# Relation stage: the order in which VectorE compares the edges, copies the projections and copies the scores

## The chip, the cores and the metric

The kernel runs on one core of one Trainium2 chip. The metric is the device time of one execution in microseconds (us); lower is better. A core has TensorE (PE, with its weight loads shown apart as PEld), VectorE (DVE), ScalarE (ACT), GpSimd (POOL), the queue engine SyncE (SP), and 16 DMA engines. Each engine runs its own list of instructions in order, and they wait for each other through semaphores only.

## The reference, cut to what matters

A chain of four graph layers and four feed-forward layers is added onto x (1875 nodes, 256 features; 31875 edges). The change lies in the third of the eight, relational attention:

```python
def _L1_gnn_ref(x, W, attn_src, attn_dst, edge_index, edge_type):
    h_all = jnp.einsum('nf,rof->rno', x, W).reshape(r, n, h, d)      # r = 8 relations, h = 8 heads, d = 32
    h_src = h_all[edge_type, src]
    h_dst = h_all[edge_type, dst]
    scores = jnp.einsum('ehd,hd->eh', h_src, attn_src) + jnp.einsum('ehd,hd->eh', h_dst, attn_dst)
    scores = jnp.where(scores > 0, scores, NEG_SLOPE * scores)
    amax = jnp.maximum(jax.ops.segment_max(scores, dst, num_segments=n), 0.0)
    w = jnp.exp(scores - amax[dst])
    denom = jax.ops.segment_sum(w, dst, num_segments=n) + 1e-12
    w = w / denom[dst]
    msg = h_src * w[..., None]
    out = jax.ops.segment_sum(msg, dst, num_segments=n)
```

## The kernel before

The nodes lie in T = 15 tiles of P = 128. The edges, sorted by tile of their destination, lie in EC = 264 chunks of 128. `relational_attention` runs its parts one after the other: `layernorm`, `relation_scores` (the one that changes), a release of semaphores with a barrier of all engines, a read of one number, `relation_rows`, and then one of two ways of attending. The number, `o.unfit`, tells whether the edges are ordered so that the segment maximum can be taken by scans in order (`attend_in_order`); it is zero here.

`relation_scores` does two things that share nothing but the engines.

- **Scores of the nodes.** SyncE loads the weights `w` (2 MB) and the heads. TensorE multiplies them in 32 products (L1843) into `p_proj`; VectorE copies that to `proj` (L1880). Then for each of 15 node tiles TensorE makes `p_score` out of two products (L1851), two banks in turn, and VectorE empties a bank with two copies (L1887, L1888). A tile waits for the two copies of the tile before the last.
- **Order of the edges.** VectorE writes each edge's key into `spread` (L1876). TensorE turns it round in 26 windows (L1832), ScalarE copies the result to `turned` (L1861, seven copies), and TensorE picks the keys just outside each window into `p_near` (L1835, L1836). VectorE then compares neighbours in `turned`: which key is smaller than the one before it (L1883), the sum of those (L1891), which equals the one before it (`o.same`, L1892), four comparisons and two sums on 26 columns (L1894 to L1900), and the masks `o.first_run` (L1903) and `o.last_run` (L1904). Semaphore `counted` is raised after the sums; TensorE, behind its last score product, waits for it and adds the three sums over the lanes (L1855). VectorE copies that (L1906) and makes `o.unfit` of it (L1908).

The order of the work is the order in which each engine's instructions are written; no scheduler moves anything. `v.drain()` makes VectorE wait for its own writes. TensorE's list is: window turns, near keys, projections (after `w_in` and `heads_in`), scores (after `proj_ready`), sums (after `counted`). GpSimd makes an index row (L1821) and issues four scatters of the adjacency (L489); it issues 132 more in `relation_rows`, paced there by TensorE. SyncE's next load, the turned weights of `relation_rows` (L1941), stands behind the barrier.

Of the kernel before, what the change touches and what calls it, by code (L numbers as in the profile page):

```python
# [9 lines left out]
ALU = mybir.AluOpType  # L10
ACT = mybir.ActivationFunctionType
AX = mybir.AxisListType

P = 128
N = 1875
D = 256
T = (N + P - 1) // P
# [9 lines left out]
R = 8  # L27
HD, DH = 8, 32
# [1753 lines left out]
def relation_scores(nc, g, xt, w, attn_src, attn_dst, score_src, score_dst, o):  # L1782


    S2 = 2 * HD
    W, L, PADS = Windows.COUNT, Windows.LANES, Windows.PADS
    sets = [range(a, min(a + 4, W)) for a in range(0, W, 4)]
    with Phase(nc, "rel") as ph:
        w_sb = ph.sb("w", [P, R, 2, D])
        heads = ph.sb("heads", [P, 2, S2])  # L1790
        proj = ph.sb("proj", [P, 2, R, S2])
        p_proj = ph.ps("p_proj", [P, 2, R, S2])
        p_score = [ph.ps(f"p_score{b}", [P, 512]) for b in range(2)]
        blanked, heads_in, w_in = ph.sem("blanked"), ph.sem("heads_in"), ph.sem("w_in")
        proj_done, proj_ready, score_done, score_taken = (ph.sem(s) for s in ("proj_done", "proj_ready", "score_done", "score_taken"))
        chunk, lift = ph.sb("chunk", [P, EC + PADS]), ph.sb("lift", [P, EC])
        spread, turned = ph.sb("spread", [P, EC + PADS, HD]), ph.sb("turned", [L, W, P])
        drop_sum, near = ph.sb("drop_sum", [L, 3]), ph.sb("near", [L, 2, W])
# [64 lines left out]
        @block.vector  # L1863
        def _(v):
            nc.vector.memset(heads[:, :, :], 0.0).then_inc(blanked, 1)
            v.wait_ge(chunk_made, 1)
            nc.vector.tensor_scalar(lift[:, :], chunk[:, 0:EC], 1.0 / 1024, P + 0.5, ALU.mult, ALU.add)
            v.drain()
            nc.vector.scalar_tensor_tensor(lift[:, :], g.dst[:, :], 0.0, lift[:, :], ALU.is_lt, ALU.mult)
            nc.vector.memset(spread[:, 0:1, :], -5.0)  # L1870
            nc.vector.tensor_scalar(spread[:, EC + 1:EC + PADS, :], chunk[:, EC + 1:EC + PADS].unsqueeze(2).to_broadcast([P, PADS - 1, HD]),
                                    float(1 << 16), None, ALU.add)
            v.drain()
            nc.vector.scalar_tensor_tensor(lift[:, :], g.tile_of[:, :], float(P), lift[:, :], ALU.mult, ALU.add)
            v.drain()
            nc.vector.tensor_tensor(spread[:, 1:EC + 1, :], g.dst[:, :].unsqueeze(2).to_broadcast([P, EC, HD]),  # L1876
                                    lift[:, :].unsqueeze(2).to_broadcast([P, EC, HD]), ALU.add).then_inc(keyed, 1)
            nc.vector.memset(o.same[:, :, :], 0.0)
            v.wait_ge(proj_done, 1)
            nc.vector.tensor_copy(proj[:, :, :, :], p_proj[:, :, :, :]).then_inc(proj_ready, 1)  # L1880
            v.wait_ge(key_copied, len(sets))
            now, earlier = turned[:, :, 1:P], turned[:, :, 0:P - 1]
            nc.vector.tensor_tensor(o.first_run[:, :, 0:P - 1], now, earlier, ALU.is_lt)  # L1883
            for t in range(T):
                v.wait_ge(score_done, t + 1)
                both = p_score[t % 2][:, 0:R * S2].rearrange("p (r s) -> p r s", r=R)
                nc.vector.tensor_copy(score_src[:, t, :, :], both[:, :, 0:HD]).then_inc(score_taken, 1)  # L1887
                nc.vector.tensor_copy(score_dst[:, t, :].rearrange("p (r h) -> p r h", r=R), both[:, :, HD:S2]).then_inc(score_taken, 1)  # L1888
            v.wait_ge(neared, 1)
            nc.vector.tensor_copy(near[:, :, :], p_near[:, :, :])  # L1890
            nc.vector.tensor_reduce(drop_sum[:, 0:1], o.first_run[:, :, 0:P - 1], AX.XY, ALU.add)  # L1891
            nc.vector.tensor_tensor(o.same[:, :, 1:P], now, earlier, ALU.is_equal)  # L1892
            v.drain()
            nc.vector.tensor_tensor(crossed[:, 0, :], turned[:, :, 0], near[:, 0, :], ALU.is_lt)  # L1894
            nc.vector.tensor_tensor(crossed[:, 1, :], near[:, 0, :], near[:, 1, :], ALU.is_equal)
            nc.vector.tensor_tensor(o.joined[:, :, 0], turned[:, :, 0], near[:, 0, :], ALU.is_equal)
            nc.vector.tensor_tensor(o.joined[:, :, 1], turned[:, :, P - 1], near[:, 1, :], ALU.is_equal)
            v.drain()
            nc.vector.tensor_reduce(drop_sum[:, 1:2], crossed[:, 0, :], AX.X, ALU.add)
            nc.vector.tensor_reduce(drop_sum[:, 2:3], crossed[:, 1, :], AX.X, ALU.add)  # L1900
            v.drain()
            v.sem_inc(counted, 1)
            nc.vector.tensor_tensor(o.first_run[:, :, :], turned[:, :, :], turned[:, :, 0:1].to_broadcast([L, W, P]), ALU.is_equal)  # L1903
            nc.vector.tensor_tensor(o.last_run[:, :, :], turned[:, :, :], turned[:, :, P - 1:P].to_broadcast([L, W, P]), ALU.is_equal)  # L1904
            v.wait_ge(drops_added, 1)
            nc.vector.tensor_copy(total[:, :], p_total[:, :])  # L1906
            v.drain()
            nc.vector.tensor_reduce(o.unfit[:, :], total[:, :], AX.X, ALU.max)  # L1908
# [627 lines left out]
```

## Time and profile before

| | us |
|---|---|
| median of 3 runs | 4527.47 |
| lowest, highest run | 4523.1, 4533.64 |
| the profiled execution, its own time | 4526.65 |
| span of the profiled execution, first to last instruction | 4525.0 |
| `relation_scores` in it, from its first instruction to its last | 2270.3 to 2335.7 |
| TensorE busy in the whole span | 2865.0 |
| VectorE busy in the whole span | 2207.9 |

The profile shows one execution. A timeline row is a start, a duration and an instruction (or a merged run of like ones, x8); the brackets behind it say how long the engine had been idle and what it had waited for. The parts of the layer are closed by barriers, so a part's length is set by whichever engine ends last in it, and the next part starts for all engines together.

### The profile page before, as it was taken

Reading aid. Unit: us, or ns where it says so; the run is one execution under the profiler, and the core shown is the slowest. Engines: PE = TensorE matmul, PEld = TensorE weight load, DVE = VectorE, ACT = ScalarE, POOL = GpSimd, SP = SyncE. Lnnn points to the kernel's source line nnn. Section 1 sums busy time; section 2 is a strip of 40 time slices with the busy share of each in tenths; the row PEclk is TensorE's granted clock in tenths of the full one; section 3 lists DMA queues with packets and bytes.
Section 4 is the critical chain, followed back from the end, with each engine's and each line's share of the span. In section 5 each row is a group of like instructions: output and inputs, shape, how many; then the busy total and the mean of one; then the engine's idle time right before and its main releaser. Section 6 shows DMA issues by size and latency. Waiting matters only on the chain. (4 is left out here: it accounts for less than half of the span.)

```text
span 4525.0 us, 52039 instructions
## 1 busy us (share of the span) xinstructions
PE 2865.0 (63%) x16062; PEld 2374.0 (52%) x16063; DVE 2207.9 (49%) x4940; ACT 726.2 (16%) x1635; POOL 1870.5 (41%) x1982
## 2 busy tenths in 40 slices
PE   3566657775777667750568256767769639947492
PEld 2456545563565455540557123336758639936391
DVE  7566645554555545566246556771254421144213
ACT  1122112221222212210112000002210113300120
POOL 4566456664666366636315666711100020020212
PEclk8788877877777777875769566667979869968696
DMA  5733223332333233313423133317756459945693
GB/s 129 287 87 88 68 67 90 90 84 59 88 89 90 53 90 89 90 34 130 161 54 109 41 92 93 94 43 254 245 185 234 157 183 327 309 149 171 210 338 119
DMA packets 358089, 607.55 MB, mean 134 GB/s; under 512 B 82185, under 2 KB 240187, under 8 KB 355131
## 3 DMA queue, kind: packets, MB, share of 16 engines
q1 hardware_dynamic: 245816, 357.76, 24.3%
q0 software_dynamic: 88640, 214.25, 17.0%
q10 hardware_dynamic: 23363, 32.26, 2.0%
q8 instruction: 130, 2.13, 0.2%
q14 instruction: 140, 1.15, 0.1%
HBM read 508.28 MB, written 95.81 MB: 134 GB/s over the span
## 5 line engine op out<-in xcount | busy, mean ns | idle before, releaser
L831 POOL DMA_INDIRECT gine_got<-gine_table,src x1056 | 1017.4, 963 | 561.2 <-issue 271.4
L905 PE MATMUL gine_p_sum<-gine_hot,gine_got 128*128 128x128 f32 x4224 | 782.9, 330 | 204.5 <-issue 174.0
L905 PEld LDWEIGHTS gine_p_sum<-gine_hot,gine_got 128*128 128x128 f32 x4224 | 690.2, 240 | 289.8 <-issue 266.0
L957 DVE TENSOR_TENSOR gine_got<-gine_got,gine_p_edge 128x512 f32<-128x512 f32 x528 | 360.5, 683 | 601.5 <-DMA unpack_rows<-in_edge_rows 250.7
L916 ACT ACTIVATE gine_got<-gine_got 128x512 f32<-128x512 f32 x528 | 332.2, 630 | 1309.5 <-DVE gine_got L957 946.9
L940 DVE TENSOR_TENSOR stack_acc<-stack_acc,gine_p_sum 128x256 f32 x1056 | 437.6, 414 | 43.0 <-issue 1.5
L489 POOL DMA_INDIRECT adjacency<-value,place x264 | 280.3, 1062 | 390.3 <-POOLq L54 191.4
L892 PE MATMUL gine_p_edge<-gine_w_a,edge_space 128*128 128x256 bf16 x1056 | 329.1, 326 | 98.7 <-issue 94.1
L893 PE MATMUL gine_p_edge<-gine_w_b,edge_space 128*128 128x256 bf16 x1056 | 328.7, 325 | 98.9 <-issue 85.8
L1416 PE MATMUL ffn_p_h<-ffn_xt,ffn_w 128*128 128x128 f32 x2864 | 347.7, 280 | 1.7 <-DVE ffn_xt L1468 0.5
L1416 PEld LDWEIGHTS ffn_p_h<-ffn_xt,ffn_w 128*128 128x128 f32 x2864 | 337.5, 196 | 4.6 <-issue 2.5
L1428 PE MATMUL ffn_p_y<-ffn_w,ffn_ht 128*128 128x256 f32 x1432 | 328.6, 380 | 4.1 <-DMA ffn_w<-in_L_ffn_w 4.1
L2302 PE MATMUL inorder_p_sum<-edge_space,inorder_hot 128*128 128x265 f32 x528 | 240.2, 572 | 132.3 <-DVE edge_space L2375 86.8
L2267 POOL DMA_INDIRECT edge_space<-h_table,hrow x264 | 272.7, 1033 | 123.3 <-issue 76.4
L1487 DVE TENSOR_TENSOR ffn_y<-ffn_p_y,ffn_b 128x256 f32<-128x256 f32 x112 | 47.5, 424 | 547.1 <-PE ffn_p_y L1428 547.1
L1682 PE MATMUL gcn_p_out<-gcn_h,gcn_a 128*128 128x256 f32 x1350 | 299.3, 380 | 0.0
L1453 ACT ACTIVATE ffn_ht<-ffn_p_h,ffn_b 128x128 f32<-128x128 f32 x716 | 204.2, 368 | 527.3 <-PE ffn_p_h L1416 527.2
L1428 PEld LDWEIGHTS ffn_p_y<-ffn_w,ffn_ht 128*128 128x128 f32 x1432 | 263.7, 190 | 37.7 <-DMA ffn_w<-in_L_ffn_w 6.2
L1682 PEld LDWEIGHTS gcn_p_out<-gcn_h,gcn_a 128*128 128x128 f32 x1350 | 254.4, 191 | 33.0
L1202 POOL IOTA route_e_idx<- 128x8 f32 (+1 forms) x3 | 0.4, 135 | 569.8 <-POOLq L54 569.8
L2302 PEld LDWEIGHTS inorder_p_sum<-edge_space,inorder_hot 128*128 128x128 f32 x528 | 114.5, 260 | 228.6 <-issue 225.4
L842 DVE TENSOR_TENSOR gine_hot<-iota_free,dst 128x512 f32<-128x512 f32 x264 | 181.6, 688 | 42.2 <-issue 36.9
(399 smaller groups left out, 3365.4 us busy)
## 6 DMA issues: line engine op xcount, KB each, us to landing
gcn_a<-adjacency SPq DMA_DIRECT2D x270, 320.0 KB
ffn_w<-in_L_ffn_W SPq DMA_DIRECT2D x74, 1024.0 KB
ffn_w<-in_L_ffn_w SPq DMA_DIRECT2D x60, 1024.0 KB
ffn_w<-in_L_ffn_w SPq DMA_DIRECT2D x90, 512.0 KB
adjacency<-zero_row ACTq DMA_DIRECT2D x3, 7200.0 KB
gine_got<-gine_table,src POOLq DMA_INDIRECT x1056
h_table<-score_rows SPq DMA_DIRECT2D x15, 1056.0 KB
edge_space<-dst_lines ACTq DMA_DIRECT2D x3, 2816.0 KB
```

Of the source, the lines that this page charges most:

```text
L489: pool.indirect_dma_start(self.tables[c % 2], bass.IndirectOffsetOnAxis(ap=self.place[:, c:c + 1], axis=0), self.value[:, c:c + 1], None). ...
L831: pool.indirect_dma_start(got[:, c % RING, :], None, table, bass.IndirectOffsetOnAxis(ap=rows[:, c:c + 1], axis=0)).then_inc(gathered[c % ...
L892: nc.tensor.matmul(edges, g.attrs_t[:, 2 * p + k, :], w_a[:, :], start=True, stop=False)
L893: ins = nc.tensor.matmul(edges, g.attrs_t[:, 2 * p + k, :], w_b[:, :], start=False, stop=True)
L905: ins = nc.tensor.matmul(p_sum[q % NB][:, k * D + half * P:k * D + (half + 1) * P], got[:, d % RING, half * P:(half + 1) * P], hot[:, d % ...
L916: nc.scalar.activation(got[:, a:a + 2, :], got[:, a:a + 2, :], ACT.Relu).then_inc(msg_ready, 1)
L940: nc.vector.tensor_tensor(into, into, p_sum[d // 2 % NB][:, d % 2 * D:(d % 2 + 1) * D], ALU.add).then_inc(added, 1)
L957: nc.vector.tensor_tensor(both, both, p_edge[p % NB][:, :], ALU.add).then_inc(summed, 1)
L1416: ins = nc.tensor.matmul(p_h[n % 2][m // 4][:, m % 4, :], w1_sb[:, n % 2, k, m * P:(m + 1) * P], xt[:, n % 2, k, :], start=(k == 0), stop= ...
L1428: ins = nc.tensor.matmul(p_y[n % 2][:, 0:D], ht[:, n % 2, m, :], w2_sb[:, n % 2, m, :], start=(m == 0), stop=(m == m_all - 1))
L1682: ins = nc.tensor.matmul(p_out[d][:, 0:D], a[:, n % RA, d * P:(d + 1) * P], h[:, t, :], start=(t == 0), stop=(t == T - 1))
L2302: nc.tensor.matmul(p_sum[c % SUMS][:, 0:WIDE], hot[:, c % HOTS, :], got[:, c % HELD, :], start=True, stop=True).then_inc(agg_done, 1)
```

## The change

In VectorE's list of `relation_scores`, the comparisons, sums and masks (L1883, L1890 to L1904) now stand directly behind the memset of `o.same` (L1878), ahead of the copy of the projections (L1880) and of the 30 score copies (L1887, L1888). Inside the moved block three things differ: a `drain` stands between L1883 and the sum over it, the sum and the equality come ahead of the wait for `neared`, and the copy of `p_near` stands behind that wait. No instruction is added or taken away except for that drain. No other engine's list changes.

```diff
             nc.vector.memset(o.same[:, :, :], 0.0)
-            v.wait_ge(proj_done, 1)
-            nc.vector.tensor_copy(proj[:, :, :, :], p_proj[:, :, :, :]).then_inc(proj_ready, 1)
             v.wait_ge(key_copied, len(sets))
             now, earlier = turned[:, :, 1:P], turned[:, :, 0:P - 1]
             nc.vector.tensor_tensor(o.first_run[:, :, 0:P - 1], now, earlier, ALU.is_lt)
+            v.drain()
+            nc.vector.tensor_reduce(drop_sum[:, 0:1], o.first_run[:, :, 0:P - 1], AX.XY, ALU.add)
+            nc.vector.tensor_tensor(o.same[:, :, 1:P], now, earlier, ALU.is_equal)
+            v.wait_ge(neared, 1)
+            nc.vector.tensor_copy(near[:, :, :], p_near[:, :, :])
+            v.drain()
...
+            v.sem_inc(counted, 1)
+            nc.vector.tensor_tensor(o.first_run[:, :, :], turned[:, :, :], turned[:, :, 0:1].to_broadcast([L, W, P]), ALU.is_equal)
+            nc.vector.tensor_tensor(o.last_run[:, :, :], turned[:, :, :], turned[:, :, P - 1:P].to_broadcast([L, W, P]), ALU.is_equal)
+            v.wait_ge(proj_done, 1)
+            nc.vector.tensor_copy(proj[:, :, :, :], p_proj[:, :, :, :]).then_inc(proj_ready, 1)
             for t in range(T):
                 v.wait_ge(score_done, t + 1)
                 both = p_score[t % 2][:, 0:R * S2].rearrange("p (r s) -> p r s", r=R)
                 nc.vector.tensor_copy(score_src[:, t, :, :], both[:, :, 0:HD]).then_inc(score_taken, 1)
                 nc.vector.tensor_copy(score_dst[:, t, :].rearrange("p (r h) -> p r h", r=R), both[:, :, HD:S2]).then_inc(score_taken, 1)
-            v.wait_ge(neared, 1)
-            nc.vector.tensor_copy(near[:, :, :], p_near[:, :, :])
-            nc.vector.tensor_reduce(drop_sum[:, 0:1], o.first_run[:, :, 0:P - 1], AX.XY, ALU.add)
-            nc.vector.tensor_tensor(o.same[:, :, 1:P], now, earlier, ALU.is_equal)
...
             v.wait_ge(drops_added, 1)
             nc.vector.tensor_copy(total[:, :], p_total[:, :])
```

VectorE's list around the copy of the projections, before (`rel_proj` is that copy, `rgat_in_score_src` and `rgat_in_score_dst` are the score copies, 15 of each, `rel_turned` the turned keys):

```order
L1876 TENSOR_TENSOR rel_spread<-dst,rel_lift 128x2112
L1878 MEMSET rgat_same_run 96x3354
L1880 COPY rel_proj<-rel_p_proj 128x256
L1883 TENSOR_TENSOR rgat_first_run<-rel_turned 96x26x127
L1887 COPY rgat_in_score_src<-rel_p_score 128x64
L1888 COPY rgat_in_score_dst<-rel_p_score 128x64
```

The same place now, from the memset on:

```order
L1876 TENSOR_TENSOR rel_spread<-dst,rel_lift 128x2112
L1878 MEMSET rgat_same_run 96x3354
L1881 TENSOR_TENSOR rgat_first_run<-rel_turned 96x26x127
L1883 TENSOR_REDUCE rel_drop_sum<-rgat_first_run 96x1
L1884 TENSOR_TENSOR rgat_same_run<-rel_turned 96x26x127
L1886 COPY rel_near<-rel_p_near 96x52
L1888 TENSOR_TENSOR rel_crossed<-rel_turned,rel_near 96x26
L1889 TENSOR_TENSOR rel_crossed<-rel_near 96x26
L1890 TENSOR_TENSOR rgat_joined<-rel_turned,rel_near 96x26
L1891 TENSOR_TENSOR rgat_joined<-rel_turned,rel_near 96x26
```

The projection copy has moved down behind this block. The rest of the block and the copy, as they now stand on VectorE:

```order
L1893 TENSOR_REDUCE rel_drop_sum<-rel_crossed 96x1
L1894 TENSOR_REDUCE rel_drop_sum<-rel_crossed 96x1
L1897 TENSOR_TENSOR rgat_first_run<-rel_turned 96x3328
L1898 TENSOR_TENSOR rgat_last_run<-rel_turned 96x3328
L1900 COPY rel_proj<-rel_p_proj 128x256
L1904 COPY rgat_in_score_src<-rel_p_score 128x64
L1905 COPY rgat_in_score_dst<-rel_p_score 128x64
```

Five long instructions (L1881, L1883, L1884, L1897, L1898) now stand ahead of the copy instead of none. The end of VectorE's list in this stage, before:

```order
L1899 TENSOR_REDUCE rel_drop_sum<-rel_crossed 96x1
L1900 TENSOR_REDUCE rel_drop_sum<-rel_crossed 96x1
L1903 TENSOR_TENSOR rgat_first_run<-rel_turned 96x3328
L1904 TENSOR_TENSOR rgat_last_run<-rel_turned 96x3328
L1906 COPY rel_total<-rel_p_total 1x3
L1908 TENSOR_REDUCE rgat_unfit<-rel_total 1x1
```

And now:

```order
L1904 COPY rgat_in_score_src<-rel_p_score 128x64
L1905 COPY rgat_in_score_dst<-rel_p_score 128x64
L1907 COPY rel_total<-rel_p_total 1x3
L1909 TENSOR_REDUCE rgat_unfit<-rel_total 1x1
L54 UNCONDITIONAL_BRANCH
```

Nothing but the copy of the sums and the final maximum stands between the last score copy and the end of the stage.

## Rows read from the trace of the kernel before

**Rows 1.** The page's head: the span of the profiled execution.
```profile
span 4525.0 us, 52039 instructions
```
**Rows 2.** Timeline up to the projections: start us, us, engine, line, operation, [idle before].
```profile
2275.31 2.85 DVE L1878 MEMSET rgat_same_run<- 96x3354 f32 x1 [0.65 <-issue]
2278.92 1.46 ACT L1861 COPY rel_turned<-rel_p_key 96x512 f32<-96x512 f32 x3 [0.25 <-PE rel_p_key L1832]
2292.03 0.46 PE L1836 MATMUL rel_p_near<-ident,rel_spread 128*96 128x1 f32 x2
2292.35 13.81 PE L1843 MATMUL rel_p_proj<-rel_heads,rel_w 128*128 128x16 f32 x64
2306.20 0.42 DVE L1880 COPY rel_proj<-rel_p_proj 128x256 f32<-128x256 f32 x1 [28.04 <-PE rel_p_proj L1843]
2306.54 3.58 DVE L1883 TENSOR_TENSOR rgat_first_run<-rel_turned 96x3302 f32<-96x3302 f32 x1
```
**Rows 3.** Timeline of the score products and their copies.
```profile
2306.68 2.08 PE L1851 MATMUL rel_p_score<-rel_proj,rgat_in_xt 128*128 128x128 f32 x8 [0.52 <-DVE rel_proj L1880]
2310.45 9.28 PE L1851 MATMUL rel_p_score<-rel_proj,rgat_in_xt 128*128 128x128 f32 x52 [1.69 <-DVE rgat_in_score_dst L1888]
2312.56 0.23 DVE L1887 COPY rgat_in_score_src<-rel_p_score 128x64 f32<-128x64 f32 x1 [0.50 <-PE rel_p_score L1851]
2313.41 0.23 DVE L1887 COPY rgat_in_score_src<-rel_p_score 128x64 f32<-128x64 f32 x1 [0.50 <-PE rel_p_score L1851]
2317.44 0.23 DVE L1887 COPY rgat_in_score_src<-rel_p_score 128x64 f32<-128x64 f32 x1 [0.31 <-PE rel_p_score L1851]
2319.76 0.23 DVE L1887 COPY rgat_in_score_src<-rel_p_score 128x64 f32<-128x64 f32 x1 [0.31 <-PE rel_p_score L1851]
```
**Rows 4.** Timeline of the stage's end: the comparisons and what waits for them.
```profile
2320.03 0.20 DVE L1890 COPY rel_near<-rel_p_near 96x52 f32<-96x52 f32 x1
2320.15 3.58 DVE L1891 TENSOR_REDUCE rel_drop_sum<-rgat_first_run 96x1 f32<-96x3302 f32 x1
2323.65 3.58 DVE L1892 TENSOR_TENSOR rgat_same_run<-rel_turned 96x3302 f32<-96x3302 f32 x1
...
2327.98 0.17 DVE L1900 TENSOR_REDUCE rel_drop_sum<-rel_crossed 96x1 f32<-96x26 f32 x1
2328.23 0.09 PEld L1855 LDWEIGHTS rel_p_total<-rel_drop_sum,ones 96*1 96x1 f32 x2 [8.69 <-DVEq L1901]
2328.23 0.19 PE L1855 MATMUL rel_p_total<-rel_drop_sum,ones 96*1 96x3 f32 x2 [8.50 <-DVEq L1901]
2328.26 3.62 DVE L1903 TENSOR_TENSOR rgat_first_run<-rel_turned 96x3328 f32<-96x3328 f32 x1
2331.80 3.62 DVE L1904 TENSOR_TENSOR rgat_last_run<-rel_turned 96x3328 f32<-96x3328 f32 x1
2335.34 0.14 DVE L1906 COPY rel_total<-rel_p_total 1x3 f32<-1x3 f32 x1
```
**Rows 5.** Busy us by stretch: PE, PEld, DVE, ACT, POOL; granted clock, DMA share, GB/s.
```profile
2280.60:2306.20 25.60, 25.57 (x160) 25.45 (x159) 0.00 (x0) 0.00 (x0) 0.00 (x0) 0.57 0.00 1
2320.00:2336.00 16.00, 0.19 (x2) 0.09 (x2) 15.36 (x14) 0.00 (x0) 0.00 (x0) 0.56 0.00 0
2315.00:2316.00 1.00, 1.00 (x9) 0.86 (x8) 0.71 (x4) 0.00 (x0) 0.00 (x0) 0.97 0.00 0
2352.00:2353.00 1.00, 1.00 (x5) 0.83 (x4) 0.00 (x0) 0.00 (x0) 0.00 (x0) 0.69 0.00 0
```
**Rows 6.** Issue and landing of the load with which the next part starts.
```profile
score_wt<-in_L_gnn_W_turned SPq DMA_DIRECT2D x1, 2048.0 KB, 7.9
```
**Rows 7.** Timeline of the next part, `relation_rows`: its products, and one pause.
```profile
2347.43 6.27 PE L1980 MATMUL score_p_rows<-score_wt,score_x_tile 128*128 128x256 f32 x16 [19.01 <-issue]
2354.52 7.10 PE L1980 MATMUL score_p_rows<-score_wt,score_x_tile 128*128 128x256 f32 x32
2383.82 0.59 ACT L2021 COPY score_rows<-score_p_rows 128x512 f32<-128x512 f32 x1 [8.35 <-DMA gather_got<-cap_results,cap_source_i]
2384.46 3.78 PE L1980 MATMUL score_p_rows<-score_wt,score_x_tile 128*128 128x256 f32 x8 [6.15 <-ACT score_rows L2021]
```

More of the change, by code:

```diff
@@ L1883, in _ @@
             nc.vector.tensor_tensor(o.first_run[:, :, 0:P - 1], now, earlier, ALU.is_lt)
[L1884 to L1888, printed above, removed]
+            v.drain()
+            nc.vector.tensor_reduce(drop_sum[:, 0:1], o.first_run[:, :, 0:P - 1], AX.XY, ALU.add)
+            nc.vector.tensor_tensor(o.same[:, :, 1:P], now, earlier, ALU.is_equal)
             v.wait_ge(neared, 1)
             nc.vector.tensor_copy(near[:, :, :], p_near[:, :, :])
-            nc.vector.tensor_reduce(drop_sum[:, 0:1], o.first_run[:, :, 0:P - 1], AX.XY, ALU.add)
-            nc.vector.tensor_tensor(o.same[:, :, 1:P], now, earlier, ALU.is_equal)
             v.drain()
@@ L1904, in _ @@
             nc.vector.tensor_tensor(o.last_run[:, :, :], turned[:, :, :], turned[:, :, P - 1:P].to_broadcast([L, W, P]), ALU.is_equal)
+            v.wait_ge(proj_done, 1)
+            nc.vector.tensor_copy(proj[:, :, :, :], p_proj[:, :, :, :]).then_inc(proj_ready, 1)
+            for t in range(T):
+                v.wait_ge(score_done, t + 1)
+                both = p_score[t % 2][:, 0:R * S2].rearrange("p (r s) -> p r s", r=R)
+                nc.vector.tensor_copy(score_src[:, t, :, :], both[:, :, 0:HD]).then_inc(score_taken, 1)
+                nc.vector.tensor_copy(score_dst[:, t, :].rearrange("p (r h) -> p r h", r=R), both[:, :, HD:S2]).then_inc(score_taken, 1)
             v.wait_ge(drops_added, 1)
```

## The prediction, made before the changed kernel had run

> **What bounds the kernel now.** I read the views in this order. The page's head gives the span, 4525.0 us [rows 1]; the layers run in sequence with barriers between their parts, so a part that ends earlier brings everything behind it forward. The reader should therefore look only at who ends last in this part. The timeline shows three stretches. In the first, VectorE has nothing to do: its memset ends at 2275.31 + 2.85 = 2278.16, and it then waits 28.04 us, until TensorE has finished the near keys and the projections at 2306.2 [rows 2]. In the second, TensorE makes the scores, to 2310.45 + 9.28 = 2319.73, with a pause of 1.69 us [rows 3]. In the third, VectorE alone works through its comparisons until it copies the sums at 2335.34 [rows 4]. The busy time by stretch says the same from the side of resources: from 2280.60 to 2306.20 TensorE is busy all of the time and VectorE, ScalarE, GpSimd and the DMA engines none of it; from 2320 to 2336 VectorE is busy 15.36 of 16 us and the others next to nothing [rows 5]. So the third stretch is bound by work whose data has been there for long: the keys were copied at 2278.92 + 1.46 = 2280.38, the near keys were ready at 2292.03 + 0.46 = 2292.49 [rows 2].
>
> **What the moved block costs in its new place.** It starts at 2280.4. The first comparison takes 3.58 (to 2284.0), the added drain and the sum another 3.6 (2287.6; 3.58, of which the row behind overlaps 0.08), the equality 3.5 (2291.2) [rows 2, 4]. Then comes the one wait that stands in a new place, for the near keys: VectorE stands 1.3 us, to 2292.5, and nobody waits for it there, since TensorE's next 13.8 us are projections that need nothing of VectorE. The near copy takes 0.2. The six small instructions end 0.92 us behind the equality (2327.98 + 0.17 less 2323.65 + 3.58), so 2293.7. The two masks take 2331.80 + 3.62 - 2328.26 = 7.2, to 2300.9 [rows 4]. The projections are complete at 2306.2. The cover is thus 5.3 us longer than what it hides, and I cost the block at nothing. If the cover failed, each microsecond past 2306.2 would delay the projection copy and with it all scores, one for one. The drain waits only for the comparison that the sum reads; no row shows one there, but the small instructions behind each other with drains between them (0.92 us in all) bound it at a few tenths, and the 5.3 us hold that. GpSimd, ScalarE and SyncE have no instruction that is moved past or held up: their DMAs and copies of this part are issued ahead of the block, and none waits for `counted`.
>
> **Term A, the scores.** Before, the first comparison (3.58 us) stood between the projection copy and the first score copy, so TensorE filled its two banks and paused 1.69 us [rows 3]. That pause goes. What becomes of the clock decides the rest. TensorE's granted clock was at its lower level, 1.2 GHz, from before the scores until about 2315.06 (the stretch 2315 to 2316 shows 0.97, so 0.06 us of it were at half) and then at 2.4 GHz [rows 5]. A tile took 0.85 us before the rise (2312.56 to 2313.41) and 0.58 after it (four tiles from 2317.44 to 2319.76) [rows 3]. The rise came 4.6 us after TensorE had taken up steady work again at 2310.45. In the next part it came 5.2 us after work began at 2347.43 (the stretch 2352 to 2353 shows 0.69, so the rise was at 2352.62) [rows 5, 7]. After the change the steady work begins at 2306.68, so I expect the rise at 2311.3 to 2311.9. By then 5.4 to 6.1 tiles are done, and the other 9.6 to 8.9 take 5.6 to 5.2 us, which gives 2316.9 to 2317.1. The same working applied to before gives 2319.46 against the 2319.73 of the row, so I add its 0.27: about 2317.3. Term A is 2319.73 - 2317.3 = 2.4 us. Bounds: if the rise stays where it was in time (2315.06), 9.9 tiles go at 0.85 and 5.1 at 0.58, the scores end at 2318.3, and A is 1.4; if the clock doesn't rise within the scores, fifteen tiles at 0.85 end at 2319.7 and A is 0. I take 2.4, by the two rises seen after steady work.
>
> A page has a say on this. The Trainium skill, "TensorE: Matmul & The Clock Gate", section "Part 1: The HAM clock gate", says that the clock rises after a time of sustained work, however many matmuls that is, and that the point varies from run to run. By it the removed pause counts double, as in my 2.4, but the rise isn't fixed to a few tenths; by row alone, with the rise left where it was, the term would be 1.4. No run yet shows which.
>
> **Term B, the tail.** Before, VectorE copied the sums 2335.34 - 2319.73 = 15.6 us after the last score product [rows 3, 4]. Now two score copies and the sum on TensorE lie between. The last score copy ended 0.38 us after the last product (2319.76 and 0.14 later its twin, of 0.21), and TensorE's sum, which before had waited 8.50 us for VectorE, takes 0.19 beside them [rows 3, 4]. The copy of the sums can start about 0.4 us behind the last product. Term B is 15.6 - 0.4 = 15.2 us.
>
> **What is late next.** After the stage everybody meets at the barrier, and the next part starts with a load of 2 MB that is issued behind it and takes 7.9 us to land [rows 6]. That load, the split of the scores and the products follow the barrier at fixed distances, and nothing was in flight from 2320 to 2336 that could still be late (0 GB/s) [rows 5]. So the whole chain shifts, and I find nothing that takes the 17.6 us back. TensorE's pause before the next part shrinks from 27.7 us (2319.73 to 2347.43) to about 12.5. The clock was down at its start before; since a pause of 6.15 us also left it down (eight matmuls in 3.78 us, against 32 in 7.10) [rows 7], I expect the same start and cost it at nothing, with 0.5 us either way.
>
> **The sum.** 2.4 + 15.2 = 17.6 us. On the profiled execution's own 4526.65 this gives 4509.05; on the median of the runs shown, 4527.47, which lies 0.8 above that, it gives 4509.9. That is 0.39% faster. With A at its bounds it would be 4510.9 or 4512.3.
>
> **The rivals.**
> - **A pause in the next part comes or goes.** ScalarE sat 8.35 us before one of its copies at 2383.82 for nothing that lies in this layer, TensorE stood 6.15 us for it, and ran the next eight matmuls in 3.78 us in place of 1.78 (8 of 7.10/32): 8.2 us in all [rows 7]. A pause of that kind may depend on how the engines stand to each other, and the start of the part shifts by 17.6 us. One more gives 4518.1, one fewer 4501.7; two more give 4526.3, which is no measurable change. Against it: all engines leave the same barrier in the same order as before. The Trainium skill, "Runtime: NRT & Kernel Launch", section "Instruction fetch mechanics", says that a taken branch whose target isn't in the window already loaded makes an engine wait for code. If these pauses are that, they hang on the loops' code, which the change leaves alone, and the time is the 4509.9 of the sum; the rows don't name the cause.
> - **The block is late.** If comparisons on VectorE run slower while TensorE is busy, the projection copy waits. The block has 17.9 us of long instructions; twice as long they would end it at about 2318.8, 12.6 us late, and 5.0 us would be left: 4522.5, no measurable change. Against it: L1883 ran beside the score products in the same 3.58 us as L1891 and L1892 ran alone [rows 2, 4].
> - **Slower: the clock in the next part.** Its 15 node tiles need 32 matmuls each: 7.10 us at 2.4 GHz, and 15.1 at the eight-in-3.78 pace, so a tile at half clock costs 8.0 us more [rows 7]. If the shorter pause ahead of the part kept the clock low longer, from 2.2 tiles on (17.6 / 8.0) the change would lose; four tiles give 4509.9 + 32 = 4541.9, slower. For it: the clock did fall while TensorE was busy (0.57 granted from 2280.60 to 2306.20) [rows 5], so work alone doesn't hold it. Against it: it rose within 5.2 us of this kind of matmul [rows 5, 7].
>
> **How the numbers follow.** The forecast with its variants of A, 4509.9 to 4512.3: 0.73. One pause fewer, 4501.7: 0.07. One more, 4518.1: 0.09. Two more, or the block late, 4522 to 4526: 0.07. Slower by the clock: 0.04. A difference under 0.2%, 9 us, can't be told from none here; that bound lies at 4518.4, so half of the 0.09 counts as no change once the runs' own spread of some 5 us is added. Faster: 0.73 + 0.07 + 0.05 = 0.85; same 0.11; slower 0.04. The range goes from 4501 to 4519: it takes in one pause more or fewer, and leaves out the last two cases.
>
> **What would show it.** In the profile after: the block lies between 2280 and 2301 with a wait of about 1.3 us for the near keys, and VectorE is idle again for about 5 us before the projection copy, which still stands 36 us behind the start of the stage. TensorE has no pause behind its second score tile and the clock rises near 2311.5, not 2315. The copy of the sums is at about 2317.7. The first product of the next part is near 2329.8, and from there each row stands about 17.6 us earlier to the end. The prediction is wrong if the projection copy moves, if the clock rises late or not at all, or if the parts behind the barrier don't keep their lengths.

## The result, and the profile after

| | before | after |
|---|---|---|
| median, us (8 runs each) | 4525.28 | 4507.47 |
| lowest, highest, us | 4513.83, 4533.64 | 4498.66, 4520.04 |
| ratio after to before, 95% interval | | 0.997 (0.9956 to 0.9984) |
| the profiled execution, own time, us | 4526.65 | 4511.05 |
| span of the profiled execution, us | 4525.0 | 4509.4 |

The changed kernel is faster by about 0.3%: the whole interval of the ratio lies below 1. The medians differ by 17.8 us; the ratio's interval, on 4525.28, says 7 to 20 us. The forecast was 4509.9, a ratio of 0.9961.

The starts of VectorE's instructions at the borders of the parts, those of its barriers included, show where the time went in the two profiled executions (us, worked out from the traces):

```
part                                   before     after   difference
everything ahead of relation_scores    2270.4    2268.9         -1.5
relation_scores                          66.2      48.3        -17.9
barrier, split of the scores              4.1       4.1          0.0
relation_rows (from the split's end)    233.7     229.5         -4.2
to attend_in_order                        3.5       4.0         +0.5
attend_in_order                         433.8     434.2         +0.4
divide_into to the end of the span     1513.3    1520.4         +7.1
```

Only the second row is the change. The others add up to +2.3, and their own spread is larger than that, as the runs below show.

The timeline of the changed kernel up to the projections, VectorE's rows but for one (the small instructions left out):

```profile
2278.92 3.60 DVE L1881 TENSOR_TENSOR rgat_first_run<-rel_turned 96x3302 f32<-96x3302 f32 x1 [2.25 <-ACT rel_turned L1861]
2282.59 3.59 DVE L1883 TENSOR_REDUCE rel_drop_sum<-rgat_first_run 96x1 f32<-96x3302 f32 x1
2286.10 3.58 DVE L1884 TENSOR_TENSOR rgat_same_run<-rel_turned 96x3302 f32<-96x3302 f32 x1
2290.86 13.81 PE L1843 MATMUL rel_p_proj<-rel_heads,rel_w 128*128 128x16 f32 x64
2291.04 0.21 DVE L1886 COPY rel_near<-rel_p_near 96x52 f32<-96x52 f32 x1 [1.35 <-PE rel_p_near L1836]
...
2292.27 3.62 DVE L1897 TENSOR_TENSOR rgat_first_run<-rel_turned 96x3328 f32<-96x3328 f32 x1
2295.81 3.62 DVE L1898 TENSOR_TENSOR rgat_last_run<-rel_turned 96x3328 f32<-96x3328 f32 x1
2304.71 0.42 DVE L1900 COPY rel_proj<-rel_p_proj 128x256 f32<-128x256 f32 x1 [5.29 <-PE rel_p_proj L1843]
```

The wait of 28.04 us before the projection copy [rows 2] has become three short ones, 2.25 for the keys, 1.35 for the near keys, 5.29 for the projections, with the block between them. The five long instructions take what they took before [rows 2, 4]. The stage's first VectorE instruction starts at 2268.86 here and at 2270.36 before, so the projection copy stands 35.84 us behind it before and 35.85 after: the block has delayed nothing. The projections themselves took 13.81 us, as before [rows 2].

The scores and the end of the stage, same view:

```profile
2305.19 10.44 PE L1851 MATMUL rel_p_score<-rel_proj,rgat_in_xt 128*128 128x128 f32 x60 [0.52 <-DVE rel_proj L1900]
...
2315.56 0.19 PE L1855 MATMUL rel_p_total<-rel_drop_sum,ones 96*1 96x3 f32 x2
2315.66 0.23 DVE L1904 COPY rgat_in_score_src<-rel_p_score 128x64 f32<-128x64 f32 x1
2315.80 0.21 DVE L1905 COPY rgat_in_score_dst<-rel_p_score 128x64 f32<-128x64 f32 x1
2315.94 0.14 DVE L1907 COPY rel_total<-rel_p_total 1x3 f32<-1x3 f32 x1
```

All 60 score matmuls (30 products, of which each leaves two records) are one run, where before there were two with 1.69 us between them [rows 3]. The 8.50 us that TensorE's sum waited and the 15.6 us of VectorE's tail [rows 4] are gone. Busy time by stretch (columns as in rows 5), the same 25.6 us as there and the second of the clock's rise:

```profile
2280.60:2306.20 25.60, 25.08 (x147) 24.98 (x147) 17.56 (x13) 0.00 (x0) 0.00 (x0) 0.54 0.00 1
2310.00:2311.00 1.00, 1.00 (x9) 0.86 (x7) 0.58 (x4) 0.00 (x0) 0.00 (x0) 0.92 0.00 0
```

VectorE, idle there before, is busy 17.56 us. The clock reached 2.4 GHz at about 2310.16 (0.92 of that microsecond), 5.0 us after the scores began.

### The profile page after: what moved, and what is told of

Same layout as the page of the kernel before. It is cut to its first block and busy times, and to the rows that moved or that the text cites. A ratio compares the mean times of both kernels' runs of the same rounds, so it can differ in the third digit from the quotient of the medians.

```text
span 4509.4 us, 52040 instructions
## 1 busy us (share of the span) xinstructions
PE 2857.9 (63%) x16062; PEld 2366.4 (52%) x16063; DVE 2208.4 (49%) x4940; ACT 726.0 (16%) x1635; POOL 1867.8 (41%) x1982
## 5 line engine op out<-in xcount | busy, mean ns | idle before, releaser
L892 PEld LDWEIGHTS gine_p_edge<-gine_w_a,edge_space 128*128 128x128 bf16 x1056 | 124.3, 118 | 150.8 <-issue 119.0
```

Of the source, the lines that this page charges most:

```text
L892: nc.tensor.matmul(edges, g.attrs_t[:, 2 * p + k, :], w_a[:, :], start=True, stop=False)
```

## The experiments

The runs of the experiments were made in four sets, beside which the kernel before had medians of 4496, 4490, 4494 and 4191 us (4525 beside the result above), so kernels of different sets are compared by their ratio to the kernel before, run beside them, and by times counted from the stage's first VectorE instruction. Kernels without an interval ran once.

### Term A: one mask back between the projection copy and the scores

```diff
-            nc.vector.tensor_tensor(o.last_run[:, :, :], turned[:, :, :], turned[:, :, P - 1:P].to_broadcast([L, W, P]), ALU.is_equal)
             v.wait_ge(proj_done, 1)
             nc.vector.tensor_copy(proj[:, :, :, :], p_proj[:, :, :, :]).then_inc(proj_ready, 1)
+            nc.vector.tensor_tensor(o.last_run[:, :, :], turned[:, :, :], turned[:, :, P - 1:P].to_broadcast([L, W, P]), ALU.is_equal)
```

> The changed kernel with one of its two masks (last_run, 3.62 us) put back between the projection copy and the first score copy; the rest of the block stays ahead. It tests term A alone. In the changed kernel the copy of the sums starts 47.1 us after the stage's first VectorE instruction. My theory (the pause goes, and the clock rises earlier because steady work starts earlier, 2.4 us together): TensorE pauses about 1.7 us after two tiles again, the clock rises about 4.6 to 5.2 us after the pause, and the copy of the sums starts at 49.5 (2.4 later). Rival (only the pause counts, the clock rises where it does in the changed kernel): 48.3 to 48.8. Rival (no effect, VectorE's copies catch up): 47.1.

Timeline of this kernel:

```profile
2287.40 0.43 DVE L1899 COPY rel_proj<-rel_p_proj 128x256 f32<-128x256 f32 x1 [8.82 <-PE rel_p_proj L1843]
2287.74 3.61 DVE L1900 TENSOR_TENSOR rgat_last_run<-rel_turned 96x3328 f32<-96x3328 f32 x1
2287.88 2.08 PE L1851 MATMUL rel_p_score<-rel_proj,rgat_in_xt 128*128 128x128 f32 x8 [0.52 <-DVE rel_proj L1899]
...
2291.68 9.71 PE L1851 MATMUL rel_p_score<-rel_proj,rgat_in_xt 128*128 128x128 f32 x52 [1.72 <-DVE rgat_in_score_dst L1905]
```

The pause is back, 1.72 us after eight matmuls. The copy of the sums came 51.8 us behind the stage's start, not 49.5: the projections themselves were 1.6 us later than in the changed kernel (37.5 against 35.85), as they were in most of the later runs, whatever stood behind them. Counted from the projection copy the distance to the copy of the sums is 14.3 us, where the theory had 13.65 and the rival without the clock 12.45 to 12.95. In the eight runs that have the scores and the sums in the changed order it lies between 10.7 and 11.7 (11.2 in the profile above), so one long instruction in that place costs 2.6 to 3.6 us, more than the 1.7 of the pause. The rest is the clock, which rose 6.0 us after work resumed there. Beside the run in which it rose about as late after steady work began (6.1 us, the loop written out, 11.7 us) the cost is 2.6. That bears out the pause and the clock together; their split isn't fixed, since the rise itself moves, and this kernel ran once.

### Term B: both masks back behind the scores

```diff
-            nc.vector.tensor_tensor(o.first_run[:, :, :], turned[:, :, :], turned[:, :, 0:1].to_broadcast([L, W, P]), ALU.is_equal)
-            nc.vector.tensor_tensor(o.last_run[:, :, :], turned[:, :, :], turned[:, :, P - 1:P].to_broadcast([L, W, P]), ALU.is_equal)
             v.wait_ge(proj_done, 1)
...
+            nc.vector.tensor_tensor(o.first_run[:, :, :], turned[:, :, :], turned[:, :, 0:1].to_broadcast([L, W, P]), ALU.is_equal)
+            nc.vector.tensor_tensor(o.last_run[:, :, :], turned[:, :, :], turned[:, :, P - 1:P].to_broadcast([L, W, P]), ALU.is_equal)
             v.wait_ge(drops_added, 1)
```

> The changed kernel with both masks (first_run, last_run) put back behind the score copies; comparisons and sums stay ahead. It tests the size of term B piece by piece. Theory (whatever VectorE does behind its last score copy lies bare on the path, one for one): the copy of the sums starts 47.1 + 7.1 = 54.2 us after the stage's first VectorE instruction, and the scores end where they do in the changed kernel (46.8). Rival (part of the tail is hidden by TensorE's sum or by the way to the barrier): below 53.

VectorE's timeline at the stage's end:

```profile
2300.31 0.21 DVE L1903 COPY rgat_in_score_dst<-rel_p_score 128x64 f32<-128x64 f32 x1
2300.44 3.61 DVE L1904 TENSOR_TENSOR rgat_first_run<-rel_turned 96x3328 f32<-96x3328 f32 x1
2303.98 3.61 DVE L1905 TENSOR_TENSOR rgat_last_run<-rel_turned 96x3328 f32<-96x3328 f32 x1
2307.51 0.14 DVE L1907 COPY rel_total<-rel_p_total 1x3 f32<-1x3 f32 x1
```

The copy of the sums stands at 54.1 us (2307.51 less the stage's start at 2253.41) against 54.2 expected, and the last score copy where it was. Work behind the last score copy counts in full.

### The cover: five masks instead of one ahead of the projections

```diff
             nc.vector.tensor_tensor(o.last_run[:, :, :], turned[:, :, :], turned[:, :, P - 1:P].to_broadcast([L, W, P]), ALU.is_equal)
+            for _ in range(4):
+                v.drain()
+                nc.vector.tensor_tensor(o.last_run[:, :, :], turned[:, :, :], turned[:, :, P - 1:P].to_broadcast([L, W, P]), ALU.is_equal)
             v.wait_ge(proj_done, 1)
```

> The changed kernel with the last mask made five times instead of once (four more, each behind a drain, same result), all in the block ahead of the projection copy. It tests the cover. In the changed kernel VectorE then idles 5.3 us before the projection copy. Theory (5.3 us of cover, then one for one): four more take 4 x 3.67 = 14.7 us, the projection copy starts 14.7 - 5.3 = 9.4 us later, at 45.2 us after the stage's first VectorE instruction instead of 35.9, and the copy of the sums at 56.5 instead of 47.1. Rival (comparisons and TensorE slow each other when they run side by side): each repeat takes clearly more than 3.62 us, or the projections take clearly more than 12.3 us, and the copy of the sums comes after 58.

```profile
2283.93 14.71 DVE L1901 TENSOR_TENSOR rgat_last_run<-rel_turned 96x3328 f32<-96x3328 f32 x4
2298.56 0.41 DVE L1903 COPY rel_proj<-rel_p_proj 128x256 f32<-128x256 f32 x1
2310.07 0.14 DVE L1910 COPY rel_total<-rel_p_total 1x3 f32<-1x3 f32 x1
```

The projection copy no longer waits; it starts 45.3 us behind the stage's start (2253.24), against 45.2 expected, and the copy of the sums 56.8 against 56.5. The repeats took 3.68 us each with their drains, 3.62 without. TensorE ran its projections from 2275.29 to 2289.10, beside the first repeat and part of the second, and stood still during the others, and all four took the same. The projections took 13.81 us, as in every profile (the 12.3 of the expectation was read off a view whose window began after they had started). So the cover is the 5.3 us that the prediction read, what lies beyond is paid one for one, and neither engine slowed the other.

### The changed kernel again, and the freed tail filled

```diff
                 nc.vector.tensor_copy(score_dst[:, t, :].rearrange("p (r h) -> p r h", r=R), both[:, :, HD:S2]).then_inc(score_taken, 1)
+            for _ in range(5):
+                v.drain()
+                nc.vector.tensor_tensor(o.last_run[:, :, :], turned[:, :, :], turned[:, :, P - 1:P].to_broadcast([L, W, P]), ALU.is_equal)
             v.wait_ge(drops_added, 1)
```

> The changed kernel itself again, five rounds beside the kernel before. Theory (17.9 us gained in relation_scores, everything behind only moved forward and otherwise different by its own spread): ratio 0.9961 (4525.3 - 17.9 over 4525.3), interval of about 0.0015 each way; relation_scores 48.3 to 50.5 us long. Rival (part of the gain is lost in the parts behind): ratio 0.998 or more, with relation_rows or attend_in_order longer than the 233.7 and 433.8 us of the kernel before.

> The changed kernel with the last mask made five times more (each behind a drain, same result) behind the score copies, which fills the freed tail with 18.4 us: the barrier comes where it came before, but the comparisons stay ahead of the scores. Theory (the gain is the bare tail and nothing else): the copy of the sums starts 65.4 us after the stage's first VectorE instruction (65.0 in the kernel before, 47.1 in the changed one) and the ratio to the kernel before is 1.000, 0.9985 to 1.0015. Rival (the other order itself changes something behind the barrier, for better or worse): the ratio stays near 0.997 or goes over 1.002.

Changed kernel again: 4475.22 us (7 runs) against 4490.5 (23 runs), ratio 0.9967 (0.9955 to 0.9978). Tail filled: 4493.39 us (11 runs), ratio 1.0003 (0.9994 to 1.0012). The tail of the kernel with the tail filled:

```profile
2300.98 0.21 DVE L1905 COPY rgat_in_score_dst<-rel_p_score 128x64 f32<-128x64 f32 x1
2301.29 18.41 DVE L1908 TENSOR_TENSOR rgat_last_run<-rel_turned 96x3328 f32<-96x3328 f32 x5
2319.62 0.14 DVE L1910 COPY rel_total<-rel_p_total 1x3 f32<-1x3 f32 x1
```

The copy of the sums stands at 66.7 us (2319.62 less 2252.94), not at the 65.4 expected: the projection copy was 1.6 us later in this run (37.5), and the fill itself took what it should. On one chip the two kernels differ by 18.5 us in the length of relation_scores (49.4 and 67.9) and by 18.2 in the median. With the tail filled nothing is left of the gain in the whole time: the gain is the shorter stage, and the order of the comparisons does nothing else that these runs can tell (the interval of its ratio leaves room for anything from 3 us less to 5 us more). The ratio 0.9967 allows a gain of 10 to 20 us, the 17.9 of the profile among them.

### What is late next: the weights of the next part

The added lines stand at the end of SyncE's list in `relation_scores`; `w_sb` is kept for `relation_rows`, which loses its own buffer and load.

```diff
+            sp.wait_ge(proj_done, 1)
+            sp.dma_start(w_sb[:, :, :, :], g.wt_src.rearrange("r (k p) o -> p (r k) o", p=P)).then_inc(g.wt_in, 16)
...
-            sp.dma_start(wt_sb[:, :, :, :], wt.rearrange("r (k p) o -> p (r k) o", p=P)).then_inc(wt_in, 16)
```

> The changed kernel with the turned weights of relation_rows loaded into the buffer of the relation weights as soon as the projections are done, and no load behind the barrier. It tests what is late next: in the changed kernel the first product of relation_rows starts 59.2 us after the stage's first VectorE instruction and follows the load. Theory (the load is last there, the split of the scores next, done at 53.5): the first product starts at 53.8, 5.4 us earlier, and the time lies about 5 us under the changed kernel. Rival (the load beside the score products slows them, or the first product follows something else): the first product stays above 57.

4470.44 us (5 runs) against 4490.5, ratio 0.995 (0.9936 to 0.9964). Its timeline around the barrier:

```profile
2296.97 0.14 DVE L1909 COPY rel_total<-rel_p_total 1x3 f32<-1x3 f32 x1
...
2302.27 1.16 DVE L332 TENSOR_TENSOR score_parts<-score_rows,score_parts 128x960 bf16<-128x960 f32 x1
2303.68 0.40 ACT L2012 COPY score_x_tile<-rgat_in_xt 128x256 f32 x1 [4.57 <-DVEq L2035]
2303.99 0.24 ACT L2020 COPY score_rows<-rgat_in_score_src 128x64 f32 x1
...
2305.11 5.21 PE L1982 MATMUL score_p_rows<-rgat_in_w,score_x_tile 128*128 128x256 f32 x16 [8.33 <-ACT score_rows L2020]
```

The load was last there: the first product starts 55.3 us behind the stage's start (2249.86) instead of 59.2, and 8.1 us behind the copy of the sums instead of 12.15 (2328.09 less 2315.94). It came at 55.3 and not at 53.8 because the split isn't next on its own. The row names ScalarE's second copy (L2020) as what TensorE waited for, but that had ended at 2304.23, 0.9 us earlier. What lay between the split's end (2302.27 + 1.16 = 2303.43) and the product is TensorE's own read of the tile numbers into registers, which I had left out; its first start is this view's 2303.7:

```profile
L788 PEldq TENSOR_LOAD <-chunk_tile x22: 4/850/875, 2303.7 to 2497.6; - x22
```

The first of them takes 0.87 us in the trace, and other register instructions follow it. From the split's end to the product it is 1.7 us here, and 1.8 and 1.7 in the two kernels below that also load early. The gain is 4 us in the profile, not 5.4. The load slowed nothing: the score products beside it took 10.43 us (10.44 in the changed kernel). The median lies 4.8 under the changed kernel's; the intervals overlap, so the runs alone don't separate the two.

### The clock at the start of the next part

In the second kernel it is 40 instead of 22.

```diff
+            for _ in range(22):
+                nc.tensor.matmul(p_rows[0][:, 0, 0:P], g.ident[:, :], g.ident[:, :], start=True, stop=True)
             pe.wait_ge(split, 1)
```

> The changed kernel with 22 matmuls of 128 columns, whose results are written over, on TensorE at the start of relation_rows while it would wait for the weights. It tests what the clock at the start of that part costs, and what a raised clock there gives. In the changed kernel the first sixteen products take 6.65 us with the clock at half until 6.0 us after they begin. Theory (steady work of about 9 us raises the clock before the products start): the first sixteen take 3.6 us and the part shortens by 3 us. Rival (the clock falls again or is not raised by these): 5.8 to 6.7 us as before and no gain.

> As the kernel with 22 extra matmuls, but with 40 of them. With 22 they took 5.15 us at the raised clock, TensorE then stood 5.05 us, the clock fell just before the products, and the first sixteen took 5.21 us. Theory (TensorE is busy up to the products, so the clock stays at 2.4 GHz): 40 take 9.4 us, TensorE stands under 1.5 us, the first sixteen products take 3.6 us, and the part is 1.6 us shorter than with 22. On the total: with 22 the kernel was slower than the changed one (0.9979 against 0.9967); if extra TensorE work itself costs time elsewhere, 40 are no better than 0.9979; if that was the run's pauses, the ratio is back at 0.9965 or less.

TensorE's timeline with 22, then with 40:

```profile
2299.95 5.15 PE L1971 MATMUL score_p_rows<-ident 128*128 128x128 f32 x44 [1.86 <-PEq L64]
2310.15 5.21 PE L1983 MATMUL score_p_rows<-score_wt,score_x_tile 128*128 128x256 f32 x16 [5.05 <-issue]
```

```profile
2299.51 10.80 PE L1971 MATMUL score_p_rows<-ident 128*128 128x128 f32 x80 [1.87 <-PEq L64]
2310.15 3.62 PE L1983 MATMUL score_p_rows<-score_wt,score_x_tile 128*128 128x256 f32 x16
```

The extra matmuls leave two records each as well. With 22 the clock was still up (1.00 from 2299 to 2309), TensorE then stood 5.05 us, and the stretch 2309 to 2314 was granted 0.66: the first sixteen products took 5.21 us. With 40 there was no pause and they took 3.62, as expected (at 22 I had expected 3.6 as well, and missed the pause behind them), against 6.65 in the changed kernel's profile and 5.89 in its second one. But the clock hadn't stayed up: it was granted 0.50 from 2300.8 to 2304.1, with TensorE busy throughout, and 1.00 from 2304.2 on, which is why the 40 took 10.80 us and not 9.4. Without extra matmuls the sixteen took between 5.21 us (weights early) and 6.66 (masks last). So the clock at the part's start is worth 1.6 to 3 us, a small thing next to the 8 us per tile of the rival, and the 5.21 with 22 is no gain that can be told from that spread.

The totals don't follow as neatly: 22 gave 0.9979 (0.997 to 0.9988), 40 gave 0.9956 (0.9943 to 0.997), the changed kernel 0.9967. The 22 matmuls cost 7.6 us against it in the same set (4482.85, 11 runs; 4475.22, 7 runs). Its profile shows one of the pauses treated next, which accounts for about 8 us of one run; whether its other runs had one too can't be seen. That extra work on TensorE costs time by itself is not borne out by the 40; why 22 are slower stays open.

### The pauses in relation_rows

```diff
-            with act.Fori(0, T // 2) as j:
+            for j in range(T // 2):
                 for p in range(2):
                     one_pass(j * 2 + p, p)
```

> The changed kernel with ScalarE's loop over the node tiles in relation_rows written out (no branch back), same work. It tests what the two pauses of ScalarE in that part are (6.89 and 7.28 us idle; TensorE stands 4.70 and 5.09 us for them and then runs eight matmuls at half clock, 2.0 us more each). Theory (ScalarE waits for its code after a taken branch): both pauses go, the part shortens from 229.5 us by about 2 x 6.9 = 13.8 to 216, and the time lies about 14 us under the changed kernel, ratio to the kernel before about 0.993. Rival (the pauses come from the data, such as the stores of h_table, whose two buffers the copies wait for): they stay at the same two copies and the time stays that of the changed kernel, ratio 0.997.

4477.06 us (5 runs) against 4496.29 (9 runs), ratio 0.9958 (0.9944 to 0.9972), and no pause of that size in its profile. That is short of the 0.993 expected and its interval overlaps that of the changed kernel, 0.9955 to 0.9978. And the test was weaker than I took it for, because the pauses turned out to differ between runs of one and the same kernel. ScalarE's pauses of over 5 us before a copy of L2021 or its counterpart in relation_rows, not counting the first copy, which waits for the part's first products, and that part's length (us):

```
kernel                       pauses    length
before                            2     233.7
after                             2     229.5
after again (same kernel)         0     215.6
one mask between                  1     221.8
masks last                        1     223.4
block long                        0     217.3
tail filled                       0     214.4
weights early                     1     216.4
22 matmuls                        1     221.9
40 matmuls                        0     214.0
loop written out                  0     215.9
loop out, weights early           0     211.1
```

The changed kernel itself had two pauses once and none the other time, and without them the part was 13.9 us shorter, 7 us for each. The row of such a pause, in the changed kernel, and what it does to TensorE:

```profile
2363.24 0.58 ACT L2022 COPY score_rows<-score_p_rows 128x512 f32<-128x512 f32 x1 [6.89 <-DMA gather_got<-cap_results,cap_source_i]
2363.88 3.78 PE L1981 MATMUL score_p_rows<-score_wt,score_x_tile 128*128 128x256 f32 x8 [4.70 <-ACT score_rows L2022]
```

The releaser named belongs to a part long over, which means that the profile doesn't know it. The Trainium skill, "Runtime: NRT & Kernel Launch", section "Instruction fetch mechanics", would have it that the engine waits for code behind a taken branch. The view of the DMA queues of the kernel before, for 2370 to 2386, in which its first pause lies (to 2383.82, 8.35 us [rows 7]), lists these queues and no instruction queue (queue: packets, MB, share):

```profile
q1 hardware_dynamic: 127, 0.94, 50.5%
q0 software_dynamic: 256, 0.00, 1.1%
```

No code was loaded in it, so that reading of the page doesn't explain this pause. The same view over the ten or eleven us up to each of the other seven pauses lists the same two queues; over the whole part (2341 to 2575) it lists two instruction queues too, with three packets, so they would have been seen. And a kernel with the loop left as it was can have none. What remains is a count: eight pauses in ten executions with the loop, none in three without it (the third is the last kernel below). One of the three, the kernel of this section, has a stand of 4.05 us with the same releaser named, just under the 5 us, for which TensorE waited 0.21 us. That fits a loop that brings them on and doesn't show it.

### Together

> The changed kernel with both ScalarE's loop of relation_rows written out and the turned weights loaded into the freed weight buffer ahead of the barrier. Alone they gave ratios to the kernel before of 0.9958 (0.9944 to 0.9972) and 0.9950 (0.9936 to 0.9964), against 0.9967 (0.9955 to 0.9978) of the changed kernel. Theory 1 (the early load gives its 4 to 5 us in each run, and the written-out loop gives nothing, since a run of the changed kernel with the loop had no pause either): 0.995 to 0.9955. Theory 2 (the loop's pauses, about 8 us each, one in a typical run, go as well): 0.9935 or less, and no pause of ScalarE over 5 us in relation_rows.

4473.31 us (5 runs) against 4494.22 (9 runs), ratio 0.9956 (0.9942 to 0.9971). relation_rows took 211.1 us, the shortest on those chips, without a pause. The ratio is 0.0001 above theory 1's range, and theory 2's 0.9935 lies outside the interval: no better than the early load alone.

The last kernel adds 20 of the matmuls to these two.

> The changed kernel with the written-out loop of ScalarE, the early load of the turned weights, and 20 extra matmuls (4.7 us at the raised clock) that bridge TensorE from the barrier to the first product. Theory: TensorE's clock stays up to the products, the first sixteen take 3.6 us, the first product starts at 55.3 to 56.5 us after the stage's first VectorE instruction (60.3 with the load behind the barrier), and relation_rows takes about 209 us (211.1 with loop and load alone, 214.0 with 40 matmuls alone, 215.6 for the changed kernel in a run without pauses). Ratio to the kernel before 0.994 to 0.9955. Rival (what is saved at the start of the part is waited for further on, since the stores and the scatters pace it): relation_rows stays at 211 or more.

4171.35 us (5 runs) against 4191.14 (9 runs), ratio 0.995 (0.9936 to 0.9964). TensorE's timeline:

```profile
2066.15 4.70 PE L1972 MATMUL score_p_rows<-ident 128*128 128x128 f32 x40 [1.86 <-PEq L64]
2072.64 3.71 PE L1984 MATMUL score_p_rows<-rgat_in_w,score_x_tile 128*128 128x256 f32 x16 [1.78 <-issue]
```

The clock stayed up and the sixteen took 3.71 us. The first product stands 57.1 us behind the stage's start, 0.6 more than the range expected, the projections having been 2.3 us later in that run than in the changed kernel's profile. This chip ran the kernel before in 4191 us in place of about 4490, and relation_rows in 189.9, so its lengths can't be set beside the others, and the rival of this kernel stays undecided; the ratio can, and it is that of the early load alone. The kernels with the early load beat the kernel before clearly, and the changed kernel by a margin that is inside the intervals.

## Why the prediction was right

**The bound.** That the end of the stage was VectorE's own work whose data had been there for long is shown by the filled tail (1.0003) and by the masks moved back (54.1 us for 54.2).

**The block in its new place.** Predicted from 2280.4 to 2300.9 with a wait of 1.3 us and 5.3 us of cover; in the profile 2278.92 to 2299.43 (1.5 us earlier, like the whole stage), 1.35 and 5.29. The added drain left 0.07 us between the comparison and its sum. The block_long kernel shows the price beyond the cover.

**Term A**, predicted 2.4, measured (2319.73 - 2270.36) - (2315.63 - 2268.86) = 2.6. The pause went and the rise came 5.0 us after steady work began, between the 4.6 and 5.2 that I had read. This was closer than the method deserves. In other runs of the same order the rise came 2.9 us (changed kernel again) and 6.1 us (loop written out) after it, and the way from the projection copy to the copy of the sums was 10.7, 11.2 and 11.7 us. With these runs term A would have been 2.1 to 3.2, so its bounds should have been at least that wide, and two rises in one trace don't give them; the prediction's own bounds, 0 and 1.4, allowed for less only, and its "counts double" was 2.4 against 1.4. The remark of the Trainium skill, "TensorE: Matmul & The Clock Gate", section "Part 1: The HAM clock gate", that the point of the rise varies from run to run is borne out. The 0.5 us either way that it gives for this is too little here: 2.9 to 6.1 us.

**Term B**, predicted 15.2, measured 15.6 - 0.3 = 15.3: the copy of the sums starts 0.31 us behind the last score product.

**Nothing takes it back.** True for relation_rows: 12.15 us from the copy of the sums to the first product against 12.1 before. I had given 0.5 us either way for the first products; they took 6.65 us against 6.27, 0.4 more. Of the +7.1 us from divide_into to the end nothing can be put down to the change: that stretch took 1512.5 to 1520.4 us in all thirteen traces (1513.3 before, 1520.4 and 1516.0 in the changed kernel), and there is one trace of the kernel before. A loss of a few us there would fit the ratios, 0.997 and 0.9967 where 0.9961 was forecast, and so would none. That stays open.

**The rivals.** The late block and the low clock did not come about; the clock's whole worth at that place is 3 us at most. Pauses do come and go, 7 us each, so that rival describes the spread of the runs of both kernels, and not something that the change sets off. I had tied it to the shift of the barrier; the same kernel showed two and none without any shift.

## What to carry to other kernels

Where a stage ends with one engine working alone on data that has been there for long, and the same engine stood idle earlier for another's result, move that work into the idle time: the gain can be read beforehand from starts in the timeline, as the bare tail less what must still follow. Count the room in the idle time with every wait that the work itself brings along (here 20.5 of 25.8 us), since each microsecond beyond it is paid in full. Parts behind a barrier keep their lengths, but their own spread between runs (here 14 us in one of them) can be as large as the gain, so judge such a change by the length of its stage first and by the total second.

## What the runs showed of the hardware

- TensorE's granted clock fell to 1.2 GHz while TensorE was busy without a break: it had 25.57 of 25.60 us of work, first the near keys and then the projections, and was granted 0.57 on average [rows 5]. It rose again during the score products.
- The clock's moves come at other moments in each run and move the stage. In the changed kernel's profile it was granted 1.00 from 2276.1 to 2282.8, 7.2 to 13.9 us behind the stage's start, with about 0.5 on both sides of that; when the kernel was run again, only from 2257.8 to 2261.1, 10.2 to 13.5 us behind it. The near keys were ready at 22.1 and 23.8 us, and the projection copy stood at 35.85 and 37.5.
- The long VectorE comparisons (3.58 to 3.62 us) were not slowed by TensorE's matmuls beside them, nor these by them (projections 13.81 us with VectorE idle and with it busy).
- Behind its last wait TensorE takes 1.6 to 1.9 us to its first product in relation_rows, 0.87 of it a read of numbers into registers (L788), which the timeline doesn't show; in the profile with the weights early it stands as a wait for ScalarE's copy.
- ScalarE can stand 6.9 to 8.4 us before a copy of TensorE's finished products, without a code load, in some executions of a kernel and not in others. The cause is open.
- One chip ran the same kernel in 4191 us; in the other sets it took 4490 to 4525. Not every part was faster there: divide_into to the end took 1520.2 us, as elsewhere. The changed kernel's ratio agreed between its two sets to 0.0003 (0.997 and 0.9967).
